# LayerNorm's application moved from VectorE to GpSimd in a two-layer Macaron block, with a new order of work

## The reference

```python
def _layernorm(x, axis=-1, eps=1e-05):
    m = jnp.mean(x, axis=axis, keepdims=True)
    v = jnp.var(x, axis=axis, keepdims=True)
    return (x - m) / jnp.sqrt(v + eps)
...
    x = x + 0.5 * _L0_ffn_ref(_layernorm(x, axis=-1), ...)
    x = x + _L0_attn_ref(_layernorm(x, axis=-1), ...)
    x = x + 0.5 * _L0_ffn_ref(_layernorm(x, axis=-1), ...)
    x = x + 0.5 * _L1_ffn_ref(_layernorm(x, axis=-1), ...)
    x = x + _L1_attn_ref(_layernorm(x, axis=-1), ...)
    x = x + 0.5 * _L1_ffn_ref(_layernorm(x, axis=-1), ...)
```

## Time and profile before

| | us |
|---|---|
| median of 3 runs | 672.85 |
| lowest and highest | 668.99, 674.85 |
| profiled execution | 674.1 |
| its span, first to last instruction | 672.3 |

### The profile page before, as it was taken

The page is one execution under the profiler, slowest core; times in us unless marked ns, Lnnn a source line. Parts: engine busy times, 40 slices in busy tenths (PEclk is TensorE's granted clock), DMA queues, the critical chain, the costliest instruction groups (busy, mean ns, idle before and its releaser), DMA issues.

```text
span 672.3 us, 14271 instructions
## 1 busy us (share of the span) xinstructions
PE 581.4 (86%) x5706; PEld 321.7 (48%) x5706; DVE 520.2 (77%) x902; ACT 361.6 (54%) x548; POOL 246.3 (37%) x239
## 2 busy tenths in 40 slices
PE   2889649989987889899999989999797998999986
PEld 1355325535544444455556455554354553554553
DVE  5989998899876978976797977977476877577352
ACT  4725215665544635566555755764465545467432
POOL 6654543273431372532222442204212442013143
PEclk9999956999978989899999999999798999999999
DMA  9500110122121020211201021120211002221311
GB/s 355 211 5 6 55 48 2 24 78 54 54 62 28 15 69 17 69 26 24 56 25 42 18 54 49 20 51 6 63 36 35 8 10 54 73 43 23 80 38 40
DMA packets 30802, 34.02 MB, mean 51 GB/s; under 512 B 9696, under 2 KB 24416, under 8 KB 30456
## 3 DMA queue, kind: packets, MB, share of 16 engines
q1 hardware_dynamic: 30736, 33.11, 17.5%
HBM read 13.82 MB, written 2.36 MB: 24 GB/s over the span
## 4 chain that ended last, share of the span: by engine, by line
PE 45%; DVE 17%; SPq 11%; DMA 8%; ACT 7%; issue 6%; POOL 6%; POOLq 0%; DVEq 0%; ACTq 0%
PE PS L510 10%; PE PS L619 8%; PE PS L528 6%; SPq L398 4%; ACT PB L733 3%; PE PS L580 3%; PE PS L601 3%; DVE XN L768 3%; DMA RB<-scratch 3%; SPq L425 3%; PE PS L546 3%; SPq L441 2%; PE PS L634 2%; DMA scratch<-DC 2%; DVE MX L923 2%
## 5 line engine op out<-in xcount | busy, mean ns | idle before, releaser
L733 ACT ACTIVATE PB<-PS 128x1024 f32<-128x1024 f32 x160 | 159.2, 1023 | 56.7 <-PE PS L460 55.7
L923 DVE TENSOR_REDUCE MX<-PS 128x2 f32<-128x1024 f32 (+2 forms) x192 | 156.9, 859 | 16.4 <-PE PS L460 16.0
L990 POOL TENSOR_TENSOR HH<-TH,HH 128x512 f16<-128x512 f32 (+1 forms) x96 | 105.6, 1112 | 157.2 <-ACT HH L692 157.0
L510 PE MATMUL PS<-XT,WGU 128*128 128x512 f16 x640 | 153.4, 386 | 4.0 <-DVE TH L874 2.3
L510 PEld LDWEIGHTS PS<-XT,WGU 128*128 128x128 f16 x640 | 57.5, 99 | 76.2 <-issue 8.1
L460 PE MATMUL PS<-MASKM,MASKW 64*128 64x128 bf16 (+1 forms) x1280 | 85.4, 212 | 0.0
L580 PE MATMUL PS<-SK,SQ 54*128 54x256 f16 (+3 forms) x512 | 65.6, 317 | 22.6 <-DVE TH L864 8.6
L619 PE MATMUL PS<-PB,V 128*32 128x512 f32 (+3 forms) x1024 | 82.5, 466 | 1.9 <-ACT PB L733 1.8
L601 PE MATMUL PS<-SQ,SK 55*128 55x384 f16 (+3 forms) x512 | 63.9, 311 | 23.2 <-DMA SQ<-NM 13.7
L528 PE MATMUL PS<-WD,HH 128*128 128x256 f16 x640 | 82.1, 278 | 2.0 <-POOL HH L990 2.0
L460 PEld LDWEIGHTS PS<-MASKM,MASKW 64*128 64x128 bf16 x1280 | 60.1, 99 | 28.7 <-issue 5.2
(11 more groups left out here) (87 smaller groups left out, 741.7 us busy)
## 6 DMA issues: line engine op xcount, KB each, us to landing
SQ<-QPB SPq DMA_DIRECT2D x96, 64.0 KB, 2.6
OC<-OT SPq DMA_DIRECT2D x64, 64.0 KB, 2.4
RB<-scratch SPq DMA_DIRECT2D x64, 64.0 KB, 2.2
SK<-QPB SPq DMA_DIRECT2D x48, 64.0 KB, 2.6
HX<-HH SPq DMA_DIRECT2D x64, 32.0 KB, 1.9
out<-X SPq DMA_DIRECT2D x4, 512.0 KB, 2.6
PB<-wd SPq DMA_DIRECT2D x2, 768.0 KB, 10.7
PB<-gu SPq DMA_DIRECT2D x2, 704.0 KB, 5.8
```

The source lines that it names most:

```text
L510: m = e.matmul(o[:, :], WGU[l][:, k, col:col + P], XT[0][j][:, k, :], start=first, stop=last)
L733: e.activation(PB[Q % 2][:, j, :, :], two_banks("s", i), ACT.Exp, scale=0.25).then_inc(a_exp, 1)
L923: e.tensor_reduce(MX[:, Q % 4, :, pr, t], o[:, :, col:col + (t + 1) * P], AX.X, ALU.max, negate=True).then_inc(a_max, 1)
L990: e.tensor_tensor(HH[1][:, s * T:s * T + wd], TH[:, i % 3, 0:wd], HH[0][:, s * T:s * T + wd], ALU.subtract).then_inc(f_lo, 1)
```

## The change

The applying instructions leave DVE's program and stand in POOL's, in the letters r and e, behind the power step. They count on semaphores of their own, f_xn and a_xn, one for each tile. The lengths LNF and LNA, which count DVE's steps, are shorter by four, and the letters X and x are gone from DVE's string. DVE's next statistics of the same kind now wait for the four applications (f_xn, a_xn), and POOL's bias addition (letter b) waits for a_xn. POOL's application waits for the transposes of the unit before (f_turn, a_turn), as DVE's did. The identity gets the semaphore l_id; X's first batch keeps l_x0. ACT's copy of the transposed tile waits for f_gate beside f_up. All strings and the banks are new.

```diff
 ORDER = {
...
     "pool":
-        "wwwwwwwwwwwrrwhwhhhhhwwdrdehhhhhhssqqssqhhdqhhhdhreddsscqeqshhqshqhshhsqdqscsqdqerhhhhhhcsscdqqdrssh"
...
+        "wwwwwwwwwrwwrwhhwhhhhwwdhrdhhhhheddhheshsqqhhhssddqqerssqhhhhqhhsdqsdqcecsqssqqcrshqhhhchhsdsqqdsrqh"
...
             if was == "load":
                 if b == 0:
-                    w.wait_ge(l_x0, 32)
+                    w.wait_ge(l_x0, 16)
...
-            e.dma_start(ID[:, :], ident).then_inc(l_x0, 16)
+            e.dma_start(ID[:, :], ident).then_inc(l_id, 16)
...
-                    w.wait_ge(l_x0, 32)
+                    w.wait_ge(l_id, 16)
                     for t in range(NT):
                         if c == "t":
-                            w.wait_ge(f_ln, LNF0[n + 1] - NT + t + 1)
+                            w.wait_ge(f_xn, NT * n + t + 1)
                         else:
-                            w.wait_ge(a_ln, LNA0[n + 1] - NT + t + 1)
+                            w.wait_ge(a_xn, NT * n + t + 1)
...
                     w.wait_ge(f_turn, i + 1)
+                    w.wait_ge(f_gate, FC * f)
                     w.wait_ge(f_up, FC * f)
...
-            def ln_apply(z, ln, xv):
-                for t in range(NT):
-                    e.tensor_scalar(XN[z][:, t, :], xv[:, t, :], MV[z][:, t, 0:1], YR[z][:, t:t + 1],
-                                    ALU.subtract, ALU.mult).then_inc(ln, 1)
...
-                    l = FFNS[i][1]
+                    b, l, _ = FFNS[i]
                     w.wait_ge(p_pool, 1)
-                    w.wait_ge(f_ln, LNF0[i + 1] - NT)
+                    w.wait_ge(f_ln, LNF0[i + 1])
...
                     e.tensor_tensor(YR[0][:, :], VE[0][:, :], HALF[:, :], ALU.pow).then_inc(f_rt, 1)
+                    w.wait_ge(f_turn, 2 * i)
+                    w.wait_ge(f_rt, i + 1)
+                    for t in range(NT):
+                        e.tensor_scalar(XN[0][:, t, :], X[:, NT * b + t, :], MV[0][:, t, 0:1], YR[0][:, t:t + 1],
+                                        ALU.subtract, ALU.mult).then_inc(f_xn, 1)
...
-                    w.wait_ge(a_ln, LNA0[NB + i + 1])
+                    w.wait_ge(a_xn, NT * (NB + i + 1))
```

More of the change, by code:

```diff
@@ L70 @@
 V0 = [0, *accumulate(NV)]
-LNF = [14 if l == 0 else 12 for _, l, _ in FFNS]
+LNF = [10 if l == 0 else 8 for _, l, _ in FFNS]
 LNF0 = [0, *accumulate(LNF)]
-LNA = [12] * NA
+LNA = [8] * NA
 LNA0 = [0, *accumulate(LNA)]
@@ L85 @@
[L85 to L89, removed]
@@ L117 @@
[L117 to L118 removed]
+        "0123456745601745236720145320415673201345167676723672014536024630460046062046720462041601246024670160"
+        "7123012463062460362406420614026426046276076420424620642704672046026407246072454062406264560202452326"
+        "7014532367204364204362046042360406340264024654026145045023023064264206452064326063267456701324604206"
+        "1010452604267042640542063452452452452064206410264120164016723012345602460246024602456024650426304620"
@@ L119 @@
+        "4260346024620645420634230101674523064216402602406214626061423614026410621607451072436047204621460246"
+        "7241624016246210462406240642602104236710764576231046246123014620671045234526043260426046230426304630"
+        "4260246304236040742062460724067245062406240624067234501624061246024016724072467017232345670167676234"
+        "5010762345101",
 }
@@ L218, in macaron_kernel @@
         p_act, p_pool, p_dve, p_pe = sem("p_act"), sem("p_pool"), sem("p_dve"), sem("p_pe")
-        f_ln, f_ve, f_mean, f_rt = sem("f_ln"), sem("f_ve"), sem("f_mean"), sem("f_rt")
+        f_ln, f_ve, f_mean, f_rt, f_xn = (sem(n) for n in ("f_ln", "f_ve", "f_mean", "f_rt", "f_xn"))
         f_turn, f_xhi, f_xlo = sem("f_turn"), sem("f_xhi"), sem("f_xlo")
@@ L773, in vector_program @@
                 at[c] += 1
-                if c in "NX":
+                if c == "N":
                     b, l, was = unit_x(i)
-                    xv = X[:, NT * b:NT * b + NT, :]
-                    if c == "N":
-                        w.wait_ge(f_ln, LNF0[i])
-                        ln_stats(0, f_ln, LNF0[i], lambda pair: wait_x(w, b, l, was, pair), xv, l == 0)
-                    else:
-                        w.wait_ge(f_turn, 2 * i)
-                        w.wait_ge(f_rt, i + 1)
-                        ln_apply(0, f_ln, xv)
-                elif c in "nx":
-                    b, l = ATT[i]
-                    xv = X[:, NT * b:NT * b + NT, :]
-                    if c == "n":
-                        w.wait_ge(a_ln, LNA0[i])
-                        ln_stats(1, a_ln, LNA0[i], lambda pair: wait_x(w, b, l, "ffn", pair), xv, False)
-                    else:
-                        w.wait_ge(a_turn, 2 * i)
-                        w.wait_ge(a_rt, i + 1)
-                        ln_apply(1, a_ln, xv)
+                    w.wait_ge(f_xn, NT * i)
+                    ln_stats(0, f_ln, LNF0[i], lambda pair: wait_x(w, b, l, was, pair), X[:, NT * b:NT * b + NT, :], l == 0)
+                elif c == "n":
+                    b, l = ATT[i]
+                    w.wait_ge(a_xn, NT * i)
+                    ln_stats(1, a_ln, LNA0[i], lambda pair: wait_x(w, b, l, "ffn", pair), X[:, NT * b:NT * b + NT, :], False)
                 elif c == "w":
@@ L984, in pool_program @@
                     e.tensor_tensor(YR[1][:, :], VE[1][:, :], HALF[:, :], ALU.pow).then_inc(a_rt, 1)
+                    w.wait_ge(a_turn, 2 * i)
+                    w.wait_ge(a_rt, i + 1)
+                    for t in range(NT):
+                        e.tensor_scalar(XN[1][:, t, :], X[:, NT * ATT[i][0] + t, :], MV[1][:, t, 0:1], YR[1][:, t:t + 1],
+                                        ALU.subtract, ALU.mult).then_inc(a_xn, 1)
                 elif c == "h":
```

56 lines of the change are left out of this document (27 added, 29 removed).

## The result

The changed kernel takes 713.65 us (median of 4 runs, 711.85 to 716.89), the kernel before 673.32 in the same comparison: ratio 1.061, 95% interval 1.0553 to 1.0667. That is 40 us slower, where 16 faster were forecast. The profiled execution took 712.4 us, its span 710.6, PE's mean granted clock 0.930 (before 0.946).

The account below looks back on a forecast made before the run. DVE was taken to bound the first 200 us and PE the rest; -14.6 - 3 + 2 + 0 + 0 = -15.6 us, from 672.85 to 657.3, forecast as 657 us, own range 649 to 665, full range 641 to 680.

Parts of the forecast that it names:

- What comes to GpSimd: 96 applying tiles on GpSimd at 500 ns each (433 to 744), 2.0 us a group, 48 us in all.
- What waits behind it: Hidden tiles' low half, rotary products, OC and residual add queue behind XN on GpSimd; one group's 2.0 us, +2 us.
- the sign that I had named: PE or ACT waits on HH, QPB or QS well above 2.0 us would speak for the slower rival.
- The chain: Statistics, power step, XN, transposes: even or slightly shorter, XN taking 2.0 us a group on POOL against 2.3 on DVE.
- The tail: Bare chain in the last unit: group ends 0.6 us later (0.3 to 1.5), costed at nothing, 1.5 in the range.
- What leaves DVE: 50.0 us of applying leaves DVE: -14.6 us from 12 to 202 us, where DVE bounds, and -3 after.
- The order: New order on all queues fills PE but may move clock and bank waits: 0, between -8 and +8 us.
- The start: First statistics 0.6 us earlier, first XN group 0.6 us longer on GpSimd: together 0 (-0.6 to +1).
- The slower one: Rival: GpSimd becomes the path in rotary stretches, 744 ns a tile, nine groups in full, 682 us; chance 0.14.
- The first rival: PE stays fed before 108 us, its clock never falls, the order takes a further 5: 645 us; chance 0.14.
- The second: Rival, nothing to measure: relief shifts PE's stalls instead of removing them, a third of 14.6 kept, 668 us; chance 0.22.
- The rule on the shared port: DVE's 48 two-input instructions (QF twice, CH) wait out GpSimd's lock: at most +24 us, a tenth expected, inside the +2.

Follow-up runs that it names:

- e6: Kernel before with pairs of single GpSimd instructions added at its end, other engines idle; half a pair of 256-column tiles with two per-partition scalars takes 1.27 us.
- e3: Changed kernel with constants in place of the two per-partition scalars in GpSimd's applying, normalization left out; 704.53 us, ratio 1.0528.
- e11: Changed kernel, GpSimd applying by two TENSOR_TENSORs (subtract, multiply) with broadcast columns, each over two tiles; 703.63 us, ratio 1.0512.
- e5: Kernel before, DVE still applying, plus four dummy tiles that nobody awaits on GpSimd behind each power step; 720.9 us, ratio 1.0765.
- e12: e2 plus four dummy tiles that nobody awaits on GpSimd behind each power step; 701.28 us, ratio 1.0457.
- e2: Changed kernel's strings and code, but DVE applies, three letters behind its statistics; 682.29 us, ratio 1.0203 to the kernel before.
- e1: Changed kernel's code with the kernel before's strings and banks, the applying letters struck from DVE's; 730.26 us, ratio 1.0915 to the kernel before.
- e18: Kernel before, DVE applying only 8 of 256 columns from the second unit of each kind on, nothing added to GpSimd; 667.2 us, ratio 0.9959.
- e20: e2 with DVE applying only 8 of 256 columns from the second unit of each kind on; 670.12 us, ratio 1.0019 to the kernel before.
- e17: e2 with single steps of DVE, ACT, POOL and SP moved a few places, PE's string and banks kept; 657.94 us, ratio 0.983 to the kernel before.

## Why the prediction was wrong, point by point

**What comes to GpSimd: the first step that failed.** I took 500 ns a tile between 433 and 744, "since one input is nearer to the first". It is 1222 in the median, 1249 and 1263 in the mean. Both bounds were rows of other operations. The lower one was a MEMSET, which reads nothing, and a four-column instruction; the upper one rested on the belief that two inputs are worse than one. e6 shows the reverse: TENSOR_SCALAR with two operations is twice TENSOR_TENSOR. So POOL got 118 us more and a group takes 4.9 us, not 2.0. That alone doesn't make up for the 57 us between forecast and result. In e3 and e11 some 17 us less of POOL's work gave 6; at that rate a tile of 500 ns, 71 us less, would have given some 25. This is a rough estimate, as the 6 is known to 5 only.

**What waits behind it, +2 taken: the second step that failed.** By e5 the load alone is worth +51 us in the old order, by e12 +17 in the change's. I had counted one group on the path because POOL was idle half of every stretch. The share misled: idle time behind the work that others await is of no use to them, and 4.9 us in front of an HH, a power step or a QS hold up ACT, SP or DVE, and in the end PE. PE's own waits on HH were 2.0 us before and after, so the sign that I had named, PE or ACT waits well above 2.0, showed less than it seems: ACT's were already 13.8 before and are 18.0 after (2.9 in e2), SP's went from 1.6 to 12.0. The other sign, a tile over 0.8 us, came true.

**The chain: even or shorter.** A bare group takes 4.9 us where four tiles on an idle DVE took 1.5, and PE waits tile by tile. From load (e12) to move (the change) it is +10 us, net of DVE's relief, and from e5 to e1 the same. The tail alone, costed at nothing with 1.5 in the range, lost 3.9 us up to the end of the transposes and 6 to the end of the program.

**What leaves DVE: -17.6.** The busy time left as forecast (DVE 473, "near 470"). Its worth was not shown: e18 found 2.7 us for 9 in the old order, e20 12, give or take 6, for 12 in the new. The argument was that a queue over 90% busy is the bound. After the change DVE is busy 75% in the first stretch, forecast above 85%, and PE did less there, as GpSimd had taken DVE's place in the chain that ended last.

**The order: 0 between -8 and +8.** By e2 it is +14 us, outside the bounds; by e17, with the same string on PE and the others remade, it is -11. The range for a wholly new order was too narrow on both sides.

**The start: 0.** The statistics started 1.9 us earlier (4.67 against 6.54), where 0.6 was forecast: X's first transfer landed sooner than the 5.2 us that I took from a median of two. The first transposes started 0.7 us earlier (11.16 against 11.85). But XN's group is 4.85 us, and the second LayerNorm's statistics now wait for it 5.34, which I had not named.

**The rivals.** The slower one was right in kind: GpSimd's in-order queue with XN in front of what others await. Its place (rotary stretches), its tile (744 ns) and so its 682 us were off; DVE's waits on QS went only from 1.1 to 3.9 us, and the waits that grew most are PE's on XN. The first rival's clock did rise in 84 to 108 us, to 0.79, and did not help; over the whole span it fell from 0.946 to 0.930. The second wanted as much idle time of PE as before: it is 34 us more. The rule on the shared port, of SBUF — State Buffer in the Trainium skill, cost nothing that can be seen: the 48 instructions took 43.5 us after and 44.2 before. QF<-QF,ROPE fell from 1176 to 953 ns in the mean, QF<-QF,QS rose from 818 to 948, CH from 793 to 822.

The loss by terms, in us; each number is the step from one kernel to the next, so the columns add up by construction:

| | forecast | strings before | the change's strings |
|---|---|---|---|
| GpSimd's load in front of other work | +2 | +51 (e5) | +17 (e2 to e12) |
| the chain, with DVE's relief | 0 and -17.6 | +10 (e5 to e1) | +10 (e12 to the change) |
| the new order | 0 | | +14 (e2) |
| together | -15.6 | +61 | +41 |

The +14 and the two +10 are known to some 5 us, and chain and relief were not parted.

## What to carry to other kernels

Before moving work to an engine, find a row of that very instruction on it (operation, number of operations, scalars) or measure it in a few instructions at the program's end; rows of other operations did not bound it here. Judge a slower in-order queue not by its busy share but by what stands right behind the moved work and how long the longest piece blocks it. And compare a move with its own order: the move cost 61 us in one order and 27 in another, while remaking the strings around the change's order on PE gave 20 to 27 us whoever applied (and nothing around the old one). Such a gain says that the order had room, not that the move was right or that it was laid out for it.

## What was not expected of the hardware

- GpSimd, 128x256 in fp32, half of a pair in e6: TENSOR_SCALAR with two operations 1.27 us with per-partition scalars, 1.12 with constants, with one operation 0.90 to 0.97; TENSOR_TENSOR 0.65.
- DVE's TENSOR_SCALAR of 128x8 takes 284 ns, of 128x256 406: the fixed part is most of it. One with 8 columns took 3075 ns, in e18, with GpSimd's WA beside it:

```profile
17.88 3.66 DVE L768 TENSOR_SCALAR XN<-X,MV,YR 128x8 f32<-128x8 f32 x4 [0.63 <-POOL YR L977]
...
18.17 3.15 POOL L966 TENSOR_TENSOR WA<-OT,WA 128x1536 f16<-128x1536 f32 x1 [0.40 <-ACT WA L662]
```

The four small instructions ended at 21.54 us, 0.2 behind GpSimd's one. SBUF — State Buffer of the Trainium skill (shared port pair) calls this an exclusive lock for a whole instruction; the trace agrees.
